# GpSimd adds the probabilities of the two heads of a pair in an instruction for each head

## The reference

```python
q = _apply_rope_subspace(q, DR)
k = _apply_rope_subspace(k, DR)
scores = jnp.einsum('bhqd,bhkd->bhqk', q, k) * scale
attn = jax.nn.softmax(scores, axis=-1)
out = jnp.einsum('bhqk,bhkd->bhqd', attn, v)
out = out.transpose(0, 2, 1, 3).reshape(b, s, H * DH)
out = out @ w_out.T + residual
```

## Time and profile before

| | |
|---|---|
| median of 3 runs | 930.24 us (927.52 to 930.43) |
| the profiled execution, its own time | 933.47 us |
| its span, first to last instruction | 931.7 us |
| PE busy | 830.1 us (89%) |
| DVE busy | 654.2 us (70%) |
| ACT busy | 389.1 us (42%) |
| POOL busy | 660.9 us (71%) |
| additions on POOL (L906) | 224, 534.7 us |
| PE's share of the chain that ended last | 74% |

### The profile page before, as it was taken

One profiled execution on the slowest core, in us unless ns is written; L12 is line 12 of the kernel. 1 busy time (PEld: TensorE's weight loads), 2 busy tenths in 40 slices (PEclk: granted clock), 3 DMA queues, 4 the chain that ended last, 5 costly groups with the idle time before them and its releaser, 6 DMA issues.

```text
span 931.7 us, 14679 instructions
## 1 busy us (share of the span) xinstructions
PE 830.1 (89%) x5118; PEld 494.6 (53%) x5118; DVE 654.2 (70%) x1172; ACT 389.1 (42%) x628; POOL 660.9 (71%) x346
## 2 busy tenths in 40 slices
PE   5767989999999999999999999999999977869671
PEld 3434445555555555555555555555555434368571
DVE  7778788667777777777777777777776767545112
ACT  3334344444444444444444444444444423336330
POOL 1488796667978787878787877878778856633323
PEclk8769899999999999999999999999999988979786
DMA  8200001001011010101010111010110000077773
GB/s 205 60 7 7 12 12 24 13 1 26 11 33 22 18 24 13 24 13 24 13 25 13 24 13 24 13 25 13 14 22 13 14 12 1 23 252 257 237 240 87
DMA packets 84330, 43.91 MB, mean 47 GB/s; under 512 B 57632, under 2 KB 73376, under 8 KB 84192
## 3 DMA queue, kind: packets, MB, share of 16 engines
q1 hardware_dynamic: 83232, 40.86, 17.4%
q0 software_dynamic: 1024, 2.10, 0.7%
HBM read 36.51 MB, written 6.16 MB: 46 GB/s over the span
## 4 chain that ended last, share of the span: by engine, by line
PE 74%; DVE 12%; issue 5%; POOL 4%; DMA 2%; ACT 1%; SPq 1%; POOLq 0%; DVEq 0%; ACTq 0%
PE ps_o L446 23%; PE ps_m L412 8%; PE ps_x L400 8%; PE ps_s L430 6%; PE ps_s L432 6%; PE ps_s L436 6%; PE ps_s L434 5%; PE ps_s L463 3%; DVE mx L1063 3%; PE ps_s L454 3%; PE ps_s L576 2%; PE ps_s L585 1%; DMA moe<-xs_dram 1%; DVE hn L1170 1%; POOL xs_dram L920 1%
## 5 line engine op out<-in xcount | busy, mean ns | idle before, releaser
L906 POOL TENSOR_TENSOR acc<-acc,probs 128x1024 f32<-128x1024 f32 (+1 forms) x192 | 459.1, 2391 | 88.1 <-ACT probs L671 66.5
L1063 DVE TENSOR_REDUCE mx<-ps_m 128x2 f32<-128x1024 f32 x240 | 293.7, 1224 | 93.6 <-PE ps_m L412 93.2
L671 ACT ACTIVATE probs<-ps_s 128x1024 f32<-128x1024 f32 x256 | 249.5, 1024 | 156.9 <-PE ps_s L436 156.2
L446 PE MATMUL ps_o<-probs,c_all 128*64 128x512 f32 x1024 | 251.7, 613 | 0.0
L412 PE MATMUL ps_m<-k_hi,q_hi 64*128 64x512 f32 x480 | 109.7, 452 | 20.0 <-DVE mx L1063 19.5
L906 POOL TENSOR_TENSOR acc<-probs 128x1024 f32<-128x1024 f32 (+1 forms) x32 | 75.6, 2362 | 63.5 <-ACT probs L671 63.2
L430 PE MATMUL ps_s<-q_hi,k_hi 64*128 64x512 f32 x512 | 104.2, 403 | 12.0 <-DVE x_sb L1110 10.9
L446 PEld LDWEIGHTS ps_o<-probs,c_all 128*64 128x64 f32 x1024 | 62.8, 137 | 94.5 <-issue 48.2
L412 PEld LDWEIGHTS ps_m<-k_hi,q_hi 64*128 64x128 f32 x480 | 46.6, 185 | 110.2 <-issue 98.7
L432 PE MATMUL ps_s<-q_hi,k_lo 64*128 64x512 f32 x512 | 102.3, 395 | 0.0
L436 PE MATMUL ps_s<-neg_row,one_row 64*128 64x512 f32 x512 | 101.7, 393 | 0.0
(11 more groups left out here) (275 smaller groups left out, 1046.8 us busy)
## 6 DMA issues: line engine op xcount, KB each, us to landing
probs<-in_experts SPq DMA_DIRECT2D x15, 578.0 KB
rr<-rd_dram SPq DMA_DIRECT2D x62, 128.0 KB
wu<-in_wqk SPq DMA_DIRECT2D x16, 256.0 KB, 3.2
neg_row<-nm SPq DMA_DIRECT2D x256, 0.5 KB, 2.0
w_first<-in_experts SPq DMA_DIRECT2D x5, 578.0 KB
rot<-in_experts SPq DMA_DIRECT2D x5, 578.0 KB
hT<-in_experts SPq DMA_DIRECT2D x5, 578.0 KB
xs_dram<-zero SPq DMA_DIRECT2D x2, 960.0 KB, 6.1
```

Source lines behind the costliest of these rows:

```text
L446: ins = nc.tensor.matmul(ps_o[64 * h:64 * h + 64, :], c_all[:, (p // HP) * TB + kt, :], probs[:, st % 4, h, :], start=(kt == 0), stop=(kt ...
L671: nc.scalar.activation(probs[:, st % 4, :, :], ps_s[:, 2 * (st % 2):2 * (st % 2) + 2, :], ACT.Exp, scale=SCALE).then_inc(s["probs"], 1)
L906: V.tensor_tensor(acc[:, half, heads, :], first, probs[:, st % 4, heads, :], ALU.add).then_inc(s["added"], 1)
L1063: V.reduce_max(mx[:, :, kh, qt], max_banks(q, n), AX.X).then_inc(s["max_reduced"], 1)
```

## The change

Where GpSimd added both heads' probabilities of a step in one instruction over `[:, heads, :]`, it now runs a loop over the heads with an instruction for each. In the second half of the last pair `heads` holds one head, so nothing differs there. The semaphore `added` counts once a step, with the last instruction of the step; the waits ahead of a step are the same, and none stands between its two instructions.

```diff
                 else:
                     first = acc[:, half, heads, :]
                     pool.wait_ge(s["added"], n_add(p, st) - 1)
-                V.tensor_tensor(acc[:, half, heads, :], first, probs[:, st % 4, heads, :], ALU.add).then_inc(s["added"], 1)
+                for h in range(heads.stop):
+                    ins = V.tensor_tensor(acc[:, half, h, :], first[:, h, :], probs[:, st % 4, h, :], ALU.add)
+                ins.then_inc(s["added"], 1)
```

## The result

| | before | after |
|---|---|---|
| median of 8 runs each, same chip | 928.17 us (927.05 to 930.43) | 925.83 us (922.63 to 926.47) |
| ratio, 95% interval | | 0.9967 (0.9952 to 0.9983) |
| profiled execution, own time (span) | 933.47 (931.7) | 922.63 (920.7) |
| first exponential of pair 0's step 2 to that of pair 15's step 14 | 733.90 | 730.67 |

A forecast was written before the change was run, and what follows sets the result against it. PE was taken to bound the kernel, with POOL's added work covered. 2.7 + 1.0 + 1.3 + 0.8 - 0.2 - 0.2 = 5.4 us less, from the median 930.24 to 924.8 us, range 920 to 932.

The forecast's parts named there:

- the prediction's own signs of being wrong: Wrong if the period of the steady halves grows, or if pairs 0 to 3 keep their length.
- Direct cost of POOL, 0: All additions: each step 0.13 us dearer, 28 us more of POOL, covered by its idle time, so 0 for the kernel.
- Not let in between halves: Rival, all halved additions: VectorE can't pass between halves and meets one 2.51 us block; 931 us, no change; chance 0.2.
- Steady halves, 0.2 lost: Steady halves, pairs 3 to 14: division waits for the third addition's end, PE's slack just covers it; 0.2 us lost, up to 2.5.
- The slower rival: Steady halves: a dearer step makes the division stall PE, loss from step 2.66; 934.0 us at step 2.80; chance 0.1.
- Pair 0, 2.7 gained: Pair 0's normalisations: first group ends 3.2 us earlier, second gives back 0.6; gain 2.7 (0.8 to 4).
- Pair 1, 1.0: Pair 1's division behind L853: passes at L853's end or loses its whole wait; gain 1.0 us (-1.5 to 2.2).
- Pair 3, 1.3: Pair 3's division: slips into a gap between additions or waits only for a first half; gain 1.3 us.
- the better of the two cases named: Pair 3: the division slips into the gap between the second and third additions, and 1.6 to 1.9 us are back.
- Pair 14, 0.8: Pair 14: division freed at the third addition's first half, PE's 0.72 us wait gone, later places 0.1; gain 0.8 together.
- Pair 15, 0.2 lost: Pair 15's expert choice: each wait halves, but fewer instructions pass and the train ends later; 0.2 us lost.

The follow-up runs named there:

- the last experiment: Additions halved in pairs 0, 1, 3, 14 and 15 only, pair 0's weight split three steps later, against the kernel before: 927.88 against 935.49 us, ratio 0.9929.
- the five pairs: Additions halved in pairs 0, 1, 3, 14 and 15 alone, whole elsewhere, against the kernel before: 929.72 against 936.44 us, ratio 0.9935.
- first whole: As the changed kernel, but each steady half's first addition whole again, measured against the kernel before: 931.65 against 935.91 us, ratio 0.9940.
- those five variants: Against before: halves outside the steady stretch 0.9933; first whole 0.9940; the five pairs 0.9935, with pair 0's split one addition later 0.9925, three steps later 0.9929.

## Why the prediction was right, and where it was off

The direction held, and so did its reason: VectorE waits for shorter GpSimd instructions. The size was about half of what was predicted (2.3 to 3.1 for 5.4). That 925.83 lies so near to 924.8 is in part luck: the prediction started from a median of 930.24 of three runs, and with all eight it is 928.17. One of the prediction's own signs of being wrong came true: the period of the steady halves grew, from 22.07 to 22.20.

*Direct cost of POOL, 0:* right. The step is about 2.66 (2.65 predicted), and PE's idle time in the steady stretch is 0.15 us.

*Not let in between halves:* it fell. No division takes over 1.55, and pair 0's second group passes at the ends of halves. The Trainium skill (SBUF — State Buffer, section "SBUF: two separate sides") tells of a lock that is held for a whole instruction. The trace agrees, and shows besides that it comes free between two that follow without a pause: the four L1002 end 0.1 behind four such ends. By the Trainium skill (GPSIMD Engine Reference, "Instruction dispatch") the cores of GpSimd overlap two instructions. If the lock followed that, it would have stayed closed; here it doesn't.

*Steady halves, 0.2 lost:* the step of the prediction that failed; 3.0 are lost. The arithmetic of the division held to 0.03. The slack was read from the start of PE's matmul, and it belongs to the weight load before it: the threshold of 7.84 from the train's start (527.81 less 519.97) is about 7.71 in truth. With the 3.0 in place of the 0.2 the sum would have been 2.6. The slower rival had the right place and too high a threshold: by its own working the loss begins at a step of about 2.62 (3 x 2.62 - 0.14 = 7.72), not 2.66.

*Pair 0, 2.7 gained:* 0.86. The first group meets the pause where it was put (the third addition ends 10.46 after step 4's exponential, 10.45 predicted), but three pass there, not two, and it ends 4.1 earlier, not 3.2. With the clock that makes 6.3 at step 10. The group behind gives back 5.5, not 0.6: it takes 4.85, where 1.11 and 2.3 more were allowed. The prediction let it meet L825 and one addition; it met four GpSimd instructions. PE's clock, which averages 0.71 behind the idle of 3.63 and 1.00 behind that of 1.13, wasn't in the sum at all.

*Pair 1, 1.0:* 2.5, and 0.7 more later in the pair; 0.9 in the two profiles where the clock falls there, so 1.66 of it are luck. Of the 2.5, 2.0 lie in the step of the division, where PE's idle of 1.70 is gone. The other 0.6 lie two steps before, at a wait that the prediction didn't list: PE's idle there is 1.43 where it was 2.00. Whether L853 holds VectorE off stays open, for the division is issued just as it ends:

```profile
129.16 1.66 POOL L853 TENSOR_TENSOR sd<-sd,half_neg 128x8 f32<-128x8 f32 x1
...
130.65 0.68 DVE L1103 TENSOR_TENSOR ou<-ou,rr 128x512 f32<-128x512 f32 x1
...
130.78 1.71 POOL L907 TENSOR_TENSOR acc<-acc,probs 128x512 f32<-128x512 f32 x1
```

The division starts 0.17 before L853's end in the profile and takes its bare 0.68. But behind additions too it passes some 0.13 ahead of their end: in the steady half it is done at 301.02, 0.55 behind the end at 300.47, and needs 0.68. So this row decides nothing. What it shows is that the next half stands still, 1.71 for 1.28: the lock goes both ways. In the last experiment L853 itself starts beside a division and takes 2.10 for 1.66.

*Pair 3, 1.3:* 1.9. The division slipped into the gap, the better of the two cases named:

```profile
233.20 0.68 DVE L1103 TENSOR_TENSOR ou<-ou,rr 128x512 f32<-128x512 f32 x1
```

*Pair 14, 0.8:* 1.5. The division takes 1.55 for 2.42, and the pair's second one meets no addition (0.68, where it took 2.70 before). PE's three waits in the pair, 0.72, 1.07 and 1.00, are gone, and 1.4 of these 2.8 are given back at pair 15's first step, where its wait is 6.70 for 5.30 (why wasn't followed).

```profile
719.39 1.55 DVE L1103 TENSOR_TENSOR ou<-ou,rr 128x512 f32<-128x512 f32 x1
```

*Pair 15, 0.2 lost:* nothing gained or lost by the choice. The steps wait less each (L1204 takes 0.96, L1202 took 2.23), the six additions end later, and the sum behind the choice stands where it stood: 788.14 before and 782.95 here, 5.19 earlier, of which 5.16 were there already when the choice began.

```profile
764.12 16.26 POOL L907 TENSOR_TENSOR acc<-acc,probs 128x512 f32<-128x512 f32 x12 [3.85 <-ACT probs L671]
...
768.82 0.96 DVE L1204 TENSOR_TENSOR rt_sb<-rt_sb,rs 128x64 f32<-128x64 f32 x1
...
782.95 0.68 DVE L1112 TENSOR_TENSOR x_sb<-x_sb,ps_s 128x512 f32<-128x512 f32 x1
```

Together the places gained 6.5, net of what pairs 0 and 14 gave back, for 5.6 predicted (2.7 + 1.0 + 1.3 + 0.8 - 0.2), and the steady stretch took 3.0 for 0.2. That the places come out so near is luck as well: pair 0's 2.7 was 0.86, and pairs 1, 3 and 14 gave more than predicted. The direction and the mechanism held and one small term, taken twenty-one times, was mis-sized. What makes it faster at the ends costs it in the middle, and a version that halves the additions only where VectorE meets them (the five pairs) or spares the one whose delay counts (first whole) reaches about 0.9935 instead of 0.9967. Among those five variants (two of them with the split moved as well) the runs tell no best, and the intervals of only those two lie wholly below the change's. Pairs 3 and 14 were only read from profiles; no run has halves there alone. The 0.73 behind pair 15's step 1 isn't the change's: the same instructions give -1.15 to +0.73 there, and two kernels with whole additions -0.78 and -0.32, all in two steps behind long idles of PE, in which the clock differs.

## What to carry to other kernels

Cutting a GpSimd instruction in two (here 1024 f32 columns) halves the time for which VectorE is locked out of SBUF, and costs about 0.13 us each; make the cut where a VectorE instruction with SBUF operands is seen to wait, not in a steady loop that has found its phase. Measure slack on TensorE at the start of the weight load, since a released matmul whose load comes late takes longer (0.51 for 0.39 here) without showing a wait. After saving a wait, lay the next instructions of that engine over the other's train at their new times: what they met there took back 5.5 of pair 0's 6.3. And before a difference of 1 to 2 us between two profiles is given to a change, compare the granted clock in that stretch: here the same instructions differed by 1.66.

## What the runs showed of the hardware that was not expected

- A pair of matmuls of 512 columns takes 0.39 when its weights are loaded 0.14 or 0.23 ahead and 0.51 when they are loaded 0.03 ahead, and in the latter case PE shows no idle time: 0.13 us a half.
- Behind each end of a GpSimd instruction with the next one following directly, exactly one waiting VectorE instruction with SBUF operands passes, in the rows of pair 0. In the pause between two steps (0.14 undisturbed) two or three do, and they can stretch it to 0.51. A group of four, met by four GpSimd instructions, thus takes 4.85 for 1.11.
- PE's granted clock averaged 0.64 behind an idle of 5.24, 0.71 behind 3.63 and 1.00 behind 1.13 and 1.59. But behind one of 1.43 to 1.45 in pair 1 it was 1.00 in three profiles and 0.77 in three, with the same instructions, so the length of the idle alone doesn't decide it. Where the clock falls, an idle costs more than its length, here by 1.5 to 2.3 us.
- The lock works both ways: a half that finds a division in progress takes 1.71 for 1.28, and the small power L853 (8 columns) 2.10 for 1.66.
- An addition of 256 columns takes 0.73, of 512 1.29 and of 1024 2.37, and two of 512 end 2.51 after their start, so a cut in two costs 0.13 to 0.14.
